# Perceiver block: value sums copied four units at a time and turned once per batch, query pieces two units at a time

## What is computed

```python
x = x + _L0_xattn_ref(_layernorm(x), ctx_1024, mask, wq, wk, wv, wo)
x = x + _L1_xattn_ref(_layernorm(x), ctx_1024, ctx_1024, Wq, Wk, Wv, Wo, bo)
# inside:
attn = softmax(einsum('bnhc,bmhc->bhnm', qh, kh) * SCALE)     # 16 heads, 128 x 2048
out  = einsum('bhnm,bmhc->bnhc', attn, vh).reshape(B, QL, DIM)
return out @ Wo.T + bo
```

## Time and profile before

| | |
|---|---|
| runs | 303.33 us (302.24 to 303.79) |
| profiled execution, first to last instruction | 302.6 us |
| busy: TensorE, VectorE, ScalarE, GpSimd | 284.7, 226.9, 207.3, 71.0 us (94%, 75%, 69%, 23%) |
| chain that ended last, by engine | PE 75%, DVE 14%, DMA 3%, ACT 3%, POOL 2% |
| cross-attention of layer 0, layer 1 | about 35 to 129 us, 168 to 257 us |
| TensorE's granted clock | 0.983 on average, full in both of these stretches |

### The profile page before, as it was taken

How to read it: one execution, slowest core, us unless ns; L and a number is a source line. 1 busy time by engine, 2 the same in 40 slices (tenths; PEclk the granted TensorE clock), 3 DMA queues, 4 the chain that set the end, 5 groups by cost and what they waited for, 6 DMA issues and landing times.

```text
span 302.6 us, 10326 instructions
## 1 busy us (share of the span) xinstructions
PE 284.7 (94%) x4336; PEld 186.6 (62%) x4340; DVE 226.9 (75%) x376; ACT 207.3 (69%) x447; POOL 71.0 (23%) x140
## 2 busy tenths in 40 slices
PE   7965999999999999899999899999999999999995
PEld 6553666666767675453656567676766665436675
DVE  5864789999999985464478998988999970744583
ACT  4638489889898888723445898989989987233350
POOL 6595500020011102431021865000011020110001
PEclk9995899999999999999999999999999999999999
DMA  7984513632222280233200036422221200000000
GB/s 238 410 248 138 169 41 106 232 119 71 87 70 80 80 301 6 104 122 105 89 3 0 3 84 213 136 79 74 79 82 54 57 2 2 0 3 2 0 0 20
DMA packets 10898, 28.06 MB, mean 93 GB/s; under 512 B 2241, under 2 KB 3329, under 8 KB 10466
## 3 DMA queue, kind: packets, MB, share of 16 engines
q1 hardware_dynamic: 10776, 27.16, 27.3%
q10 hardware_dynamic: 74, 0.20, 0.2%
HBM read 20.74 MB, written 6.62 MB: 90 GB/s over the span
## 4 chain that ended last, share of the span: by engine, by line
PE 75%; DVE 14%; DMA 3%; ACT 3%; POOL 2%; issue 2%; ACTq 1%; DVEq 0%; POOLq 0%
PE bank L1082 73%; DVE mx L835 7%; DMA k_first_rows<-kparts 2%; ACT probs L557 1%; DMA kpair<-k_first_rows 1%; DVE kparts L804 1%; DVE k_rest L801 1%; DVE s_neg L894 1%; DVE st L745 1%; POOL m_rows L438 1%; PE bank L1387 1%; ACTq L276 1%; PE bank L1427 0%; DVE xn L764 0%; DVE negm L842 0%
## 5 line engine op out<-in xcount | busy, mean ns | idle before, releaser
L835 DVE TENSOR_REDUCE mx<-bank 128x2 f32<-128x1024 f32 x128 | 153.0, 1222 | 19.1 <-PE bank L1082 15.2
L557 ACT ACTIVATE probs<-bank 128x512 f32<-128x512 f32 x256 | 139.3, 595 | 20.7 <-PE bank L1082 16.7
L1082 PE MATMUL bank<-q_exp,kpair 64*128 64x128 bf16 x1024 | 84.8, 218 | 1.9 <-ACT probs L557 1.2
L1082 PE MATMUL bank<-probs,v_all 128*9 128x128 f32 x2048 | 80.1, 274 | 1.1 <-ACT probs L557 1.0
L1082 PE MATMUL bank<-kpair,q_rows 64*128 64x512 bf16 x256 | 73.9, 388 | 5.8 <-DMA kpair<-k_first_rows 5.8
L1082 PEld LDWEIGHTS bank<-q_exp,kpair 64*128 64x128 bf16 x1024 | 55.3, 94 | 31.5 <-ACT probs L557 13.2
L1082 PEld LDWEIGHTS bank<-probs,v_all 128*9 128x9 f32 x2048 | 43.2, 90 | 17.0 <-ACT probs L557 4.0
L438 POOL CAST m_rows<-negm 128x2 bf16<-128x2 f32 x32 | 7.1, 222 | 136.5 <-DVE negm L842 136.5
L1082 PEld LDWEIGHTS bank<-kpair,q_rows 64*128 64x128 bf16 x256 | 22.6, 93 | 7.9 <-issue 6.4
L494 ACT ACTIVATE v_all<-bank 128x512 f32<-128x512 f32 (+1 forms) x20 | 10.5, 538 | 11.9 <-PE bank L1082 11.9
L629 ACT ACTIVATE s_sb<-bank 128x512 f32<-128x512 f32 x16 | 8.3, 602 | 11.9 <-PE bank L1082 11.9
(11 more groups left out here) (226 smaller groups left out, 348.2 us busy)
## 6 DMA issues: line engine op xcount, KB each, us to landing
k_scratch<-kparts SPq DMA_DIRECT2D x24, 256.0 KB, 2.8
kpair<-k_scratch SPq DMA_DIRECT2D x62, 96.0 KB
kpair<-k_scratch SPq DMA_DIRECT2D x62, 64.0 KB
ctxT_s<-in_ctxT SPq DMA_DIRECT2D x4, 512.0 KB, 5.8
mask_s<-in_mask SPq DMA_DIRECT2D x2, 1024.0 KB, 10.3
kpair<-k_scratch SPq DMA_DIRECT2D x62, 32.0 KB
wM<-in_packM SPq DMA_DIRECT2D x1, 1728.0 KB, 7.0
wB<-in_packB SPq DMA_DIRECT2D x1, 599.0 KB, 4.9
```

The costliest lines, as they stand in the source:

```text
L557: act.activation(probs[:, j % 4, :], bank[:, 4 + j % 2, :], ACT.Exp).then_inc(S("exp_done"), 1)
L835: V.tensor_reduce(mx[n % 2][:, w, :], bank[:, 2 * (w % 2):2 * (w % 2) + 2, :], AX.X, ALU.max) \
L1082: return T.matmul(out_, lhsT=lhsT, rhs=rhs, start=start, stop=stop, **kw)
```

## The change

The value sums of four units in a row get four column ranges of bank 7, so `take_o` copies 512 columns at a time: in units 4, 8 and 12, then 384 columns in unit 15 and the last 128 after it (`TAKES`). `o_all` keeps eight units. `heads` goes. `sums(b)` takes its place once per batch: 16 matmuls with 32 columns of `sel_o` as the stationary operand and one unit's sums as the moving one, four column groups of the array side by side, two halves added. They give the summed heads (`o_sums`) and, repeated for each feature, the sums of exponentials (`l_sums`), both with features on partitions, in bank 6. So nothing is turned any more, `divide` takes 128 reciprocals per partition and writes `oT`, and the rows of the output weights are put in the new order of features on the host. For batch 0 ScalarE copies both to SBUF (`take_sums`, after the fifth exponential of unit 8), since bank 6 is needed; for batch 1 VectorE reads bank 6. The work for batch 0 in `X_UNIT` starts with the projection and stands one unit earlier from there on; so do VectorE's and GpSimd's parts of it. `place_pieces` does two pieces in the even units 0 to 6 with one copy of 256 columns.

Left out below: the changed offsets in the second weight pack (110 columns more), the semaphore counts, `take_x`, `make_x` and `wait_x`, and GpSimd's two shifted unit numbers.

```diff
@@ -75,7 +75,10 @@
 SUF_BANK = 2
-X_UNIT = (9, 10, 12, 13, 14, 15)
+X_UNIT = (9, 11, 12, 13, 14)
+TAKES = {4: (0, 4), 8: (4, 8), 12: (8, 12), 15: (12, 15)}
+N_TAKES = len(TAKES) + 1
+PIECES = (0, 2, 4, 6)
@@ -121,9 +124,9 @@
         probs = sb("probs", [P, 4, 512])
-        o_sb = [sb(f"o_sb{i}", [P, P]) for i in range(2)]
-        o_rec = sb("o_rec", [P, B, H])
-        onorm = sb("onorm", [P, B, P])
+        o_all = sb("o_all", [P, NP, P])
+        ol_sb = sb("ol_sb", [P, 2 * P])
+        o_rec = sb("o_rec", [P, P])
@@ -212,14 +215,13 @@
         ones_row = R_("ones")
-        sel_o = B_("sel_o", 18)
+        sel_o = B_("sel_o", 128)
...
-        def heads_ps(b):
-            return bank[:, 6 + b, 256:256 + H * 9].rearrange("p (h c) -> p h c", c=9)
+        o_sums, l_sums = bank[:, 6, 2 * P:3 * P], bank[:, 6, 3 * P:4 * P]
@@ -546,9 +552,19 @@
-                def take_o(n):
-                    act.wait_ge(S("pv_done"), 4 * (g0 + n + 1))
-                    copy(o_sb[n % 2][:, :], bank[:, 7, 0:P]).then_inc(S("o_taken"), 1)
+                def take_o(first, end):
...
+                    act.wait_ge(S("pv_done"), 4 * (g0 + end))
+                    if l or first >= NP:
+                        act.wait_ge(S("o_summed"), 2 * l + first // NP)
+                    a, w = first % NP, end - first
+                    copy(o_all[:, a:a + w, :], bank[:, 7, first % 4 * P:(first % 4 + w) * P]
+                         .rearrange("p (u q) -> p u q", q=P)).then_inc(S("o_taken"), 1)
...
+                def take_sums():
...
+                    act.wait_ge(S("o_summed"), 2 * l + 1)
+                    copy(ol_sb[:, :], bank[:, 6, 2 * P:4 * P]).then_inc(S("ol_taken"), 1)
@@ -601,20 +615,23 @@
                         exp_unit(n, j)
-                        if j == 1 and n:
-                            take_o(n - 1)
-                        if j == 3 and n in X_UNIT and n != 10:
+                        if j == 1 and n in TAKES:
+                            take_o(*TAKES[n])
+                        if j == 4 and n == NP:
+                            take_sums()
+                        if j == 3 and n in X_UNIT and n != 9:
                             take_x(n)
-                        if l and j == 3 and n < NP:
-                            act.wait_ge(S("q_piece"), n + 1)
-                            copy(q_rows[:, n, P:2 * P], x_out).then_inc(S("q_pieced"), 1)
+                        if l and j == 3 and n in PIECES:
+                            act.wait_ge(S("q_piece"), n // 2 + 1)
+                            copy(q_rows[:, n:n + 2, P:2 * P], bank[:, 6, P:3 * P].rearrange("p (i q) -> p i q", i=2)) \
+                                .then_inc(S("q_pieced"), 1)
@@ -632,8 +649,6 @@
-                act.wait_ge(S("oT_p"), l + 1)
-                copy(oT[:, P:2 * P], bank[:, 4, 0:P]).then_inc(S("oT"), 1)
@@ -787,11 +802,13 @@
-                dve.wait_ge(S("o_heads"), NN * l + NP * (b + 1))
-                V.reciprocal(o_rec[:, b, :], heads_ps(b)[:, :, HD]).then_inc(S("o_rec"), 1)
+                if b:
+                    dve.wait_ge(S("o_summed"), 2 * l + 2)
+                else:
+                    dve.wait_ge(S("ol_taken"), l + 1)
+                V.reciprocal(o_rec[:, :], l_sums if b else ol_sb[:, P:2 * P]).then_inc(S("o_rec"), 1)
                 dve.wait_ge(S("o_rec"), B * l + b + 1)
-                V.tensor_tensor(onorm[:, b, :].rearrange("p (h d) -> p h d", h=H), heads_ps(b)[:, :, 0:HD],
-                                o_rec[:, b, :].unsqueeze(2).to_broadcast([P, H, HD]), ALU.mult) \
+                V.tensor_tensor(oT[:, b * P:(b + 1) * P], o_sums if b else ol_sb[:, 0:P], o_rec[:, :], ALU.mult) \
@@ -867,15 +884,15 @@
                         divide(l, 0)
-                    elif n == 10:
+                    elif n == 9:
...
                         V.tensor_tensor(x[:, 0, :], x_out, x[:, 0, :], ALU.add).then_inc(S("x_taken"), 1)
-                        dve.wait_ge(S("x_taken"), 3 * l + 2)
+                        dve.wait_ge(S("x_taken"), 2 * l + 1)
...
                         variance(("n1a", "n4a")[l])
-                    elif n == 11:
+                    elif n == 10:
                         rows(("n1a", "n4a")[l])
-                    elif n == 14:
+                    elif n == 13:
@@ -1167,14 +1184,16 @@
-            def place_piece(p):
+            def place_pieces(p):
...
                 r = slice(p // 2 * 32, p // 2 * 32 + 32)
-                for s in range(PARTS):
-                    c = (p % 2 * PARTS + s) * P
-                    last = mm(x_out, selq[r, c:c + P], q_parts[r, s, P:2 * P], start=(s == 0), stop=(s == PARTS - 1))
+                for i in range(2):
+                    for s in range(PARTS):
+                        c = (i * PARTS + s) * P
+                        last = mm(bank[:, 6, (1 + i) * P:(2 + i) * P], selq[r, c:c + P], q_parts[r, s, P:2 * P],
+                                  start=(s == 0), stop=(s == PARTS - 1))
@@ -1288,26 +1307,31 @@
                 def pv_group(n, k):
-                    if k == 0 and g0 + n:
-                        pe.wait_ge(S("o_taken"), g0 + n)
+                    if k == 0 and g0 + n and (n == 0 or n in TAKES):
+                        pe.wait_ge(S("o_taken"), takes(l, n))
...
                             row = (2 * a + t % 2) * 32
-                            last = mm(bank[row:row + VW, 7, 0:P], v_all[l][:, n // NP, 4 * k + t, n % NP * 2 + a, :],
+                            last = mm(bank[row:row + VW, 7, n % 4 * P:(n % 4 + 1) * P], v_all[l][:, n // NP, 4 * k + t, n % NP * 2 + a, :],
...
-                def heads(n):
...
-                    if g0 + n == 0:
+                def sums(b):
...
+                    if l == 0:
                         pe.wait_ge(S("in_B"), 16)
-                    pe.wait_ge(S("o_taken"), g0 + n + 1)
-                    mm(heads_ps(n // NP)[:, n % NP * 2:n % NP * 2 + 2, :], o_sb[n % 2][:, :], sel_o) \
-                        .then_inc(S("o_heads"), 1)
+                    pe.wait_ge(S("o_taken"), N_TAKES * (l + 1) if b else takes(l, NP))
+                    for i, out_ in enumerate((o_sums, l_sums)):
+                        for half in range(2):
+                            c = (2 * i + half) * 32
+                            for g in range(4):
+                                last = mm(out_[group(g), :], sel_o[:, c:c + 32], o_all[:, 4 * half + g, :],
+                                          start=(half == 0), stop=(half == 1))
+                    last.then_inc(S("o_summed"), 1)
@@ -1342,10 +1366,10 @@
                         b_unit(n, 2 * k + 1)
-                        if k == 1 and n:
-                            heads(n - 1)
-                        if l and k == 1 and n < NP:
-                            place_piece(n)
+                        if k == 1 and n == NP:
+                            sums(0)
+                        if l and k == 1 and n in PIECES:
+                            place_pieces(n)
@@ -1428,11 +1452,9 @@
                 scores(0)
+                keep_clock(7, 4)
+                pe.wait_ge(S("v32"), 2 * l + 1)
                 pe.wait_ge(S("o_div"), 2 * l + 2)
-                T.transpose(bank[:, 4, 0:P], onorm[:, 1, :], ident).then_inc(S("oT_p"), 1)
-                keep_clock(7, 2)
-                pe.wait_ge(S("v32"), 2 * l + 1)
-                pe.wait_ge(S("oT"), l + 1)
@@ -1616,10 +1638,13 @@
                 selq[h * HD + d, h // 2 % 2, qp, (h % 2) * HOFF + K_BASE[kp] + d * K_TIMES[kp] + qp] = one
-    sel_o = np.zeros((P, 2, 9), np.float32)
+    sel_o = np.zeros((P, 2, 2, 32), np.float32)
     for t in range(4):
-        for c in range(VW):
-            sel_o[t * 32 + c, t // 2, c] = 1.0
+        for half in range(2):
+            for d in range(HD):
+                c = 16 * half + t // 2 * HD + d
+                sel_o[t * 32 + d, 0, half, c] = 1.0
+                sel_o[t * 32 + HD, 1, half, c] = 1.0
@@ -1647,13 +1678,13 @@
     packA = np.concatenate([x[0], x[1], f["L0_xattn_wk"].reshape(P, P), ident, f["L0_xattn_wq"].reshape(P, P),
-                            f["L0_xattn_wv"].reshape(P, P), f["L0_xattn_wo"].reshape(P, P)], axis=1)
+                            f["L0_xattn_wv"].reshape(P, P), by_tile(f["L0_xattn_wo"].reshape(P, P))], axis=1)
```

More of the change, by code:

```diff
@@ L59 @@
 PK_B = dict(w_oT=0, w_uv=128, w_uk=192, wk1=256, wv1=384, wq1=512, wo1=640, aq=768, ak=896, av=1024,
-            aoT=1152, router=1280, hsel=1296, qsel=1300, sel_o=1304, bq=1322, bk=1323,
-            fill=1324, nfill=1325, upper=1326)
+            aoT=1152, router=1280, hsel=1296, qsel=1300, sel_o=1304, bq=1432, bk=1433,
+            fill=1434, nfill=1435, upper=1436)
 PK_B1_W = 256
-PK_B_W = 1454
+PK_B_W = 1564
 PK_C = dict(w_dq=0, w_uqT=128, w_dkv=256)
@@ L241, in span, with takes @@
             return slice(bs[0], bs[-1] + 1)
+        def takes(l, n):
+            return N_TAKES * l + sum(u <= n for u in TAKES)
         def x_before(l, n):
@@ L616, in cross @@
```

(17 more changed lines are left out.)

29 lines of the change are left out of this document (13 added, 16 removed).

## The result

The changed kernel takes 307.28 us (median of four runs, 306.75 to 307.90), the kernel before 302.93 with a further run beside it (four runs, 302.24 to 303.79). The ratio is 1.0116 [1.0089, 1.0143]: 3.5 us slower, between 2.7 and 4.3. So the loss is known as 3.3 to 4.4 us and no closer. The forecast was 307.2.

A forecast was written before the change was run, and what follows sets the result against it. Two latency loops across engines, the longer 5.34 us, bound the units, not TensorE's work. Span 302.6 us, with -0.33 - 0.8 + 2 x (2.28 - 0.15 - 0.5 + 0.88) = +3.89, becomes 306.5; plus 0.76, 307.2, range 304.6 to 309.2.

The forecast's parts named there:

- Steady units of layer 0 unchanged: Layer 0's steady units: TensorE's path falls from 5.27 to 4.94 us, the spacing stays 5.34, so worth 0.
- the loop: Chain of waits across engines from one unit's `put_exp` to the next, 5.34 us, said to fix the spacing of units.
- Division of batch 0: Unit 8 of each layer: the division waits some 1.6 us for new work, costing 2.28 us per layer.
- The rival of a hidden division: Unit 8's wait and longer reciprocal fall into slack: without 2 x 2.28 us, 302.6 us; chance 0.12.
- the TensorE-bound one: Rival: TensorE is the bound, so each heads call removed pays 0.33 us: 300.0 us; chance 0.12.
- The reciprocal's width: In the division, 128 columns take 0.95 us, on the line through 16 and 32 columns, 6.2 ns a column.
- Query pieces: Layer 1's spacings of 5.53 us fall to 5.34 in odd units and 5.42 in even ones: about -0.8.
- Unit 15 and the moved steps: Per layer, -0.5 us in unit 15, and -0.15 from T(10), unit 10's `negm` start, to the last `put_exp`.
- End of the stage: Each layer's end: later scores and a longer reciprocal delay the addition into x by 0.88 us.
- From the span to the median: Profiled span 302.6 us becomes 306.5; the median of the runs lies 0.76 above it, so 307.2.

The follow-up runs named there:

- e1: Changed kernel with one matmul the size of a heads call put back in step 1 of every unit but 0, 8 and 9: 309.44 us, ratio 1.0210.
- e3: Changed kernel with `put_exp` issued behind step 3's last scores and the `q_exp` copy one exponential later: 305.10 us, ratio 1.0065.
- e2: Changed kernel with the reciprocal over 16 of the 128 columns only: 304.66 us, ratio 1.0045.
- e5: Changed kernel with `take_sums` behind the fourth exponential of unit 8 instead of the fifth: 304.62 us, ratio 1.0033.
- e6: Changed kernel with layer 1's query pieces placed one per unit again instead of in pairs: 307.7 us in one run.
- e4: Kernel before with `put_exp` issued behind step 3's last scores and the `q_exp` copy one exponential later: 307.32 us, ratio 1.0133.
- e7: Changed kernel with `take_sums` one exponential earlier, division behind unit 10's first maximum, sums of exponentials first at stage's end, two `keep_clock` matmuls for four: 305.01 us, ratio 1.0063.

## Why the prediction was right

*Steady units of layer 0 unchanged: right, and shown.* From T(3) on the spacing is 5.47 once, where it was 5.48, and then 5.33 to 5.34 up to T(9). VectorE's wait before its second maximum grew from 0.17 to 0.33, and ScalarE has 0.31 and 0.21 of idle time a unit instead of 0.40. The idle time grew by less than the 0.3 a unit of the forecast: between T(7) and T(8) TensorE is busy for 5.20 us instead of 5.33 and ScalarE for 4.63 instead of 4.80. The 0.3 was the busy time taken out, and part of the matmul had lain beside its neighbours. e1 shows it from the other side. That the loop runs over `put_exp` is shown by e3, which moves only that and its copy and changes the spacing.

*Division of batch 0: right in each term.* Forecast a wait of 1.6, a reciprocal of 0.95 and a spacing of 7.6; measured 1.59, 0.95, and 7.60 and 7.51. The sums, taken at 0.95, show 1.08 as a block, with 0.87 to the value matmuls behind it here and 1.01 to the scores behind it at the stage's end. Both terms are on the path (e2, e5). The rival of a hidden division is out by the 1.59 of idle time and by e5, in which a shorter wait shortens the spacing by as much; the TensorE-bound one is out by e1.

*The reciprocal's width: right.* The 128x128 form takes 0.954 and 0.958 on average, on the line of the two narrow rows. The groups by shape in the changed kernel (mean ns of one behind the busy time):

```profile
L809 DVE RECIPROCAL o_rec<-bank 128x128 f32<-128x128 f32 x2 | 1.9, 958 | 11.2 <-PE bank L1099 11.2
L809 DVE RECIPROCAL o_rec<-ol_sb 128x128 f32<-128x128 f32 x2 | 1.9, 954 | 3.1 <-ACT ol_sb L500 3.1
```

The figure of the Trainium skill (VectorE: DVE Perf Modes, First, the fixed hardware budget) that was weighed, a repeat count of 8, gave 1.19 when read as 8 cycles a column. That reading is not what this operation shows: the measured step is 6.3 ns a column ((954 - 253) / 112). The advice of the Trainium skill to vectorize PSUM access (TensorEngine Tiling, PSUM Bottleneck) went with 2.0 us less of busy time on ScalarE and a longer kernel. The wide copies alone were not tried; that they were worth nothing is argued from the idle time that ScalarE had in every unit.

*Query pieces: the sign right, the size made of errors that in part cancel.* Forecast -0.8, measured -1.00. The forecast had the even units at 5.42 and units 2, 4 and 6 came to 5.37 to 5.46; it had 0.2 for the wide copy in unit 4, where at most 0.09 shows, and 0.08 for unit 0, where 0.17 does. e6 shows that the pairs themselves cost 0.28 of what the missing heads and copies gave.

*Unit 15 and the moved steps: small terms off.* Unit 15 gave -0.38 where -0.5 stood, the stretch from T(10) to the last `put_exp` -0.30 where -0.15 stood. Both are small beside the division.

*End of the stage: right in size, half right in its reason.* From the sums to the addition 3.56 was forecast (132.30 less 128.74) and 3.47 measured, and the two clocks agree there by chance within 0.1 (128.74 and 128.81). But the prediction had this as the price of the reciprocal's chain. e2 shows that the scores, 0.7 later, would have cost all but 0.09 of it.

*From the span to the median: right by luck.* The forecast added 3.89 to the span of 302.6, and 0.76 for the median of the runs. From T(0) on 3.33 was measured, by the ratio 3.5, by the medians 4.35, so the sum was 0.56 too high by the first and 0.46 too low by the last, and 307.2 against 307.28 says little of it. The span after is 304.7 and not 306.5: 0.56 of that is the sum, and 1.23 is start-up code that is the same in both and took less in that execution. The profiles show what that was. A row of matmuls that waits for a DMA starts at 25.27 instead of 25.95; and TensorE's granted clock, at its lower level (1.2 GHz) before, is full from 30 us on instead of from about 32, so the matmuls up to the first `negm` take 0.54 less. The executions for which both are known last about 2.0 us longer than their span, so the profiled execution of before would have taken some 304.6 (an estimate), above every one of the four runs beside it. These scatters are as large as several of the terms that were argued over.

What failed was not in the forecast but behind it: e3's size, e4's sign and e7's gain. In each the loop to be shortened had been read well, and what holds the units next was not followed through all engines: which matmul would stand on it, and whose data would come late.

## What to carry to other kernels

Before work is taken off a busy engine, find the chain from one iteration's marker to the next and see whether the work is on it: here 32 matmuls and 22 copies brought 2 to 3 us, nearly all of it in the units that no loop held, and what took their place in one burst cost some 6 (2.24 + 2.15 + 2 x 0.79). Work spread through idle gaps was free here, as long as the order kept it off the loop; the same work gathered once per batch needed a gap of its own. So put each hand-over (the copy here) where its engine stands and not behind an operation that itself waits. Compare two profiles between marks inside the loop, since start-up alone may differ by more than the effect.
